# The second norm of a GNN stack: row sums and centred squares in place of the statistics instructions, copies in another order

## What is computed

```python
def _layernorm(x, axis=-1, eps=1e-05):
    m = jnp.mean(x, axis=axis, keepdims=True)
    v = jnp.var(x, axis=axis, keepdims=True)
    return (x - m) / jnp.sqrt(v + eps)
...
    x = _layernorm(x + _L0_gnn_ref(x, adj, ...))     # masked gram matrix, rows scaled to norm 1, times values
    x = _layernorm(x + _L1_gnn_ref(x, adj, ...))     # normalized adjacency times (x @ weight), plus bias
    x = _layernorm(x + _L2_gnn_ref(x, adj, adj, ...))  # three steps of a gated update
    x = _layernorm(x + _L3_gnn_ref(x, adj, ...))     # attention with 8 heads and a mask
```

## Time and profile before

| | us |
|---|---|
| median of 3 runs | 2118.96 |
| lowest and highest | 2114.54 and 2122.32 |
| the profiled execution, its own time | 2114.17 |
| its span, first to last instruction | 2112.4 |

### The profile page before, as it was taken

One profiled execution on the slowest core, in us unless ns is written; L12 is line 12 of the kernel. 1 busy time (PEld: TensorE's weight loads), 2 busy tenths in 40 slices (PEclk: granted clock), 3 DMA queues, 4 the chain that ended last, 5 costly groups with the idle time before them and its releaser, 6 DMA issues.

```text
span 2112.4 us, 34482 instructions
## 1 busy us (share of the span) xinstructions
PE 2027.2 (96%) x12214; PEld 1632.8 (77%) x12214; DVE 1570.5 (74%) x3442; ACT 1253.7 (59%) x2501; POOL 1032.5 (49%) x1153
## 2 busy tenths in 40 slices
PE   6889999999999999999999999999999999999986
PEld 5667787877878787787877878787787877878764
DVE  5567777777777778777777777778777777877756
ACT  3335647566575656646566575656657566565745
POOL 3123645446364554545445463554535555454546
PEclk8999999999999999999999999999999999999999
DMA  4003022120211203112120212213012120302212
GB/s 135 1 20 70 21 51 51 41 71 21 57 35 48 63 22 71 39 41 51 41 71 21 64 27 57 54 31 71 30 41 51 41 71 21 70 21 61 51 47 65
DMA packets 65631, 101.14 MB, mean 48 GB/s; under 512 B 11440, under 2 KB 31152, under 8 KB 65456
## 3 DMA queue, kind: packets, MB, share of 16 engines
q1 hardware_dynamic: 65456, 98.87, 18.4%
HBM read 23.34 MB, written 8.39 MB: 15 GB/s over the span
## 4 chain that ended last, share of the span: by engine, by line
PE 88%; DVE 4%; ACT 3%; POOL 2%; issue 2%; SPq 0%; DMA 0%; POOLq 0%; DVEq 0%; ACTq 0%
PE ps L1026 18%; PE ps L1028 17%; PE ps L1027 17%; PE ps L1048 12%; PE ps L1140 10%; PE ps L1160 6%; PE ps L1124 5%; PE ps L1451 2%; ACT fa L449 1%; POOL fa L334 1%; PE ps L1220 1%; PE ps L1253 1%; POOL rsum L328 1%; DVE ra L943 0%; DVE fa L781 0%
## 5 line engine op out<-in xcount | busy, mean ns | idle before, releaser
L328 POOL TENSOR_TENSOR rsum<-esum,mhalf 128x2 f32<-128x2 f32 x256 | 209.9, 820 | 598.6 <-ACT fa L449 598.5
L334 POOL TENSOR_SCALAR fa<-fa,rsum 128x512 f32<-128x512 f32 x512 | 442.1, 875 | 54.5 <-POOL rsum L328 54.5
L781 DVE CUSTOM_DVE_ANT_0 fa<-ps,mask 128x512 f32<-128x512 f32 x512 | 332.2, 686 | 157.3 <-PE ps L1124 152.0
L449 ACT ACTIVATE fa<-fa,nmax 128x512 f32<-128x512 f32 x512 | 367.0, 725 | 48.2 <-DVE nmax L781 48.2
L444 ACT COPY pT<-ps 128x512 f32<-128x512 f32 x480 | 276.8, 583 | 150.3 <-PE ps L1140 148.5
L1140 PE MATMUL ps<-ident,fa 128*128 128x128 f32 x1920 | 287.2, 275 | 14.6 <-POOL fa L334 10.6
L1140 PEld LDWEIGHTS ps<-ident,fa 128*128 128x128 f32 x1920 | 230.4, 141 | 88.1 <-issue 22.7
L768 DVE TENSOR_TENSOR ra<-ps,ra 128x512 fp32r<-128x512 f32 x224 | 150.9, 686 | 181.8 <-ACT ra L591 94.4
L1048 PE MATMUL ps<-adjT,ra 128*128 128x512 f32 x1024 | 261.2, 405 | 8.0 <-DVE ra L943 5.2
L1048 PEld LDWEIGHTS ps<-adjT,ra 128*128 128x128 f32 x1024 | 192.5, 192 | 63.1 <-ACT pT L444 8.3
L323 POOL TENSOR_TENSOR rstd<-veps,mhalf 128x2 f32<-128x2 f32 x128 | 98.0, 771 | 167.9 <-DVE veps L748 167.9
(11 more groups left out here) (197 smaller groups left out, 4682.8 us busy)
## 6 DMA issues: line engine op xcount, KB each, us to landing
ra<-ra SPq DMA_DIRECT2D x512, 128.0 KB, 2.4
fa<-in_x_T SPq DMA_DIRECT2D x17, 512.0 KB, 4.7
fa<-in_x SPq DMA_DIRECT2D x17, 512.0 KB, 3.9
out<-fa SPq DMA_DIRECT2D x15, 512.0 KB, 3.0
fa<-in_L_gnn_w_w SPq DMA_DIRECT2D x3, 512.0 KB, 10.7
adj_n<-in_adj SPq DMA_DIRECT2D x1, 1024.0 KB, 8.1
fa<-in_L_gnn_u_w SPq DMA_DIRECT2D x2, 256.0 KB, 10.0
out<-xn SPq DMA_DIRECT2D x2, 256.0 KB, 2.1
```

What stands on the lines that cost most here:

```text
L328: nc.gpsimd.tensor_tensor(rsum[:, 2 * k:2 * k + 2], esum[:, 2 * k:2 * k + 2], mhalf[:, 4:6], ALU.pow).then_inc(rs_r, 1)
L334: nc.gpsimd.tensor_scalar(SC[:, g], SC[:, g], rsum[:, 2 * k + u:2 * k + u + 1], 1.0, ALU.mult, ALU.mult).then_inc(nrm, 1)
L449: nc.scalar.activation(SC[:, s % RING], SC[:, s % RING], ACT.Exp, bias=nmax[:, s:s + 1], scale=-1.0, accum_out=esum[:, s:s + 1]).then_inc( ...
L781: nc.vector.tensor_tensor_reduce(out=SC[:, s % RING], in0=ps[:, (4 if i is not None else lone_bank(k)) + u], in1=mask[:, 2 * (k % 8 // 4) ...
```

## The change

The second norm no longer uses the statistics instructions. `sums_and_means` lets the residual sum itself accumulate the row sum (`xsum`), and VectorE makes `nmean` = -sum / (32 D) from it. ScalarE squares x / 32 + `nmean` with an accumulator, four tiles of 128x256 into `XS` (which is free by then), so `vsum` is a quarter of the variance (256 / 1024), and VectorE adds a quarter of eps. VectorE also writes the mean into `mv` for `normalize`. Two semaphores are new: `x2_m` (nmean of a half is there) and `x2_q` (its squares are).

The order around it changes as well:

- TensorE: `qk_of(3)` ahead of `back(t, 0, 0)`; the transposes of x2's first half between `back(t, 0, 0)` and `back(t, 0, 1)`; `back(t, 0, 1)` in bank 6 in place of bank 0, so that it needs the copy of `back(t, 0, 0)`; in this gather, two more node tiles ahead of the wait for bank 1, and no wait for `prob_copy(t, 0, 1)`.
- ScalarE: squares behind `exponentials(t, 0)` and ahead of `qk_hi(2)`; both copies of x2's high words in a row, `qk_hi(3)` behind them, and `prob_copy(t, 0, 1)` behind the copies of `hT` and its high words.
- VectorE: both low-word steps of x2 in a row ahead of `qk_lo(2)`; `qk_lo(3)` behind the low words of hT; the statistics of X4 (batch o) behind the gather's low words of the first step.

```diff
--- before.py
+++ after.py
@@ -65,6 +65,10 @@
         mv = sb("mv", [P, 4, NT, 2])
         veps = sb("veps", [P, 4, NT])
         rstd = sb("rstd", [P, 4, NT])
+
+        xsum = sb("xsum", [P, NT])
+        nmean = sb("nmean", [P, NT])
+        vsum = sb("vsum", [P, NT])
         rsd = sb("rsd", [P, NT])
         ssq = sb("ssq", [P, NT])
         rnorm = sb("rnorm", [P, NT])
@@ -120,7 +124,7 @@
         ps = ctx.enter_context(nc.psum_tensor("ps", [P, 8, N], F32))
         PT_BANK, O_BANK = 6, 7
         QK_BANK = (6, 7, 1, 7)
-        CHAIN_G, CHAIN_T, CHAIN_O = 2 * 6 + 2 + 8 * STEPS, 4, 4
+        CHAIN_G, CHAIN_T, CHAIN_O = 6 + 4 + 2 + 8 * STEPS, 4, 4
 
         def pair(b):
             return ps[:, b:b + 2, :]
@@ -132,10 +136,7 @@
             return slice(2 * c, 2 * c + 2)
 
 
-
         def pt_bank(k, c):
-            if (k, c) == (0, 1):
-                return 0
             return 4 + c if k in (5, 9, 13) else PT_BANK
 
         adj_in = sem("adj_loaded"); w0_in = sem("layer_0_weights_loaded"); w2_in = sem("layer_2_weights_loaded")
@@ -166,6 +167,7 @@
         sq_f = sem("rel_squared"); ssq_ps = sem("ssq_ps"); ssq_c = sem("ssq_copied"); rn_r = sem("rnorm_ready")
         sq_s = sem("squares_summed")
         u_ps = sem("u_ps"); u_h = sem("u_h"); u_l = sem("u_l"); o_ps = sem("o_ps")
+        x2_m = sem("x2_means"); x2_q = sem("x2_squared")
         ln_v = [sem(f"var_of_norm_{k}") for k in range(4)]
         ln_r = [sem(f"rstd_of_norm_{k}") for k in range(4)]
         x1s_f = sem("x1_scaled"); x1s_h = sem("x1s_h"); x1s_l = sem("x1s_l")
@@ -554,15 +556,22 @@
                     tiles_hi(AB0, 0, t_ps, t_h)
                 if t is not None:
                     exponentials(t, 0)
+                if i is not None:
+                    for c in range(2):
+                        act.wait_ge(x2_m, i * 2 + (c + 1))
+                        for s in (2 * c, 2 * c + 1):
+                            ins = nc.scalar.activation(XS[:, s], xg[:, s], ACT.Square, bias=nmean[:, s:s + 1],
+                                                       scale=1.0 / 32, accum_out=vsum[:, s:s + 1])
+                        ins.then_inc(x2_q, 1)
+                if t is not None:
                     qk_hi(2)
                     prob_copy(t, 0, 0)
-                    qk_hi(3)
-                for c in range(2):
-                    if i is not None:
+                if i is not None:
+                    for c in range(2):
                         act.wait_ge(x2_r, i * 2 + (c + 1))
                         copy(XNS[:, H, half(c)], xg[:, half(c)]).then_inc(xn_h, 1)
-                    if t is not None and c == 0:
-                        prob_copy(t, 0, 1)
+                if t is not None:
+                    qk_hi(3)
                 if i is not None:
                     for d in range(DT):
                         act.wait_ge(hT_ps, i * 2 + (d + 1))
@@ -571,6 +580,7 @@
                         act.wait_ge(h_c, i * 2 + (d + 1))
                         copy(HTS[:, H, d], hT[:, d]).then_inc(hT_h, 1)
                 if t is not None:
+                    prob_copy(t, 0, 1)
                     exponentials(t, 1)
 
                 for j in range(STEPS):
@@ -763,6 +773,23 @@
                         after("g", mark("g", ins))
                         variance("g", k, c, aggregate("g", k, c, stats_of("g", xg, k, c)))
 
+
+
+                def sums_and_means():
+                    for c in range(2):
+                        dve.wait_ge(o1_ps, i * 2 + (c + 1))
+                        for s in (2 * c, 2 * c + 1):
+                            ins = STT(xg[:, s], natural(2)[:, s], dinv[:, s:s + 1], xg[:, s], ALU.mult, ALU.add,
+                                      accum_out=xsum[:, s:s + 1])
+                        after("g", mark("g", ins))
+                        TS(nmean[:, half(c)], xsum[:, half(c)], -1.0 / (32 * D), None, ALU.mult).then_inc(x2_m, 1)
+                    for c in range(2):
+                        n = mark("g", TS(mv[:, 1, half(c), 0], xsum[:, half(c)], 1.0 / D, None, ALU.mult))
+                    after("g", n)
+                    for c in range(2):
+                        dve.wait_ge(x2_q, i * 2 + (c + 1))
+                        TS(veps[:, 1, half(c)], vsum[:, half(c)], 0.25 * EPS, None, ALU.add).then_inc(ln_v[1], 1)
+
                 def tile_lo(dst, b, d, ready, value, signal):
                     dve.wait_ge(ready, value)
                     TT(dst[:, L, d], ps[:, b + d], f32(dst[:, H, d]), ALU.subtract).then_inc(signal, 1)
@@ -933,28 +960,24 @@
                     masked(0)
                 if i is not None:
                     dve.wait_ge(xb_r, i + 1)
-                    sums_and_statistics(1, o1_ps, dinv, xg)
+                    sums_and_means()
                 if i is not None:
                     normalize(xg, xg, 1, 0, i, x2_r)
                     normalize(xg, xg, 1, 1, i, x2_r)
-                for c in range(2):
-                    if i is not None:
+                if i is not None:
+                    for c in range(2):
                         dve.wait_ge(xn_h, i * 6 + (c + 1))
                         TT(XNS[:, L, half(c)], xg[:, half(c)], f32(XNS[:, H, half(c)]), ALU.subtract).then_inc(xn_l, 1)
-                    if t is not None and c == 0:
-                        qk_lo(2)
-                if t is not None:
+                if t is not None:
+                    qk_lo(2)
                     masked(1)
-                    qk_lo(3)
                 if i is not None:
                     for d in range(DT):
                         dve.wait_ge(hT_h, i * 6 + (d + 1))
                         TT(HTS[:, L, d], hT[:, d], f32(HTS[:, H, d]), ALU.subtract).then_inc(hT_l, 1)
                 if t is not None:
+                    qk_lo(3)
                     masked(2)
-                if o is not None:
-                    dve.wait_ge(x4a, o + 1)
-                    x4_0, x4_1 = stats_of("o", X4, 3, 0), stats_of("o", X4, 3, 1)
 
                 for j in range(STEPS):
                     A, B_, C, E = [4 * (j + 1) + k for k in range(4)]
@@ -970,6 +993,9 @@
                         m = i * 6 + 2 * j
                         for d in range(DT):
                             tile_lo(AB0, 0, d, a_h, m + (d + 1), a_l)
+                    if o is not None and j == 0:
+                        dve.wait_ge(x4a, o + 1)
+                        x4_0, x4_1 = stats_of("o", X4, 3, 0), stats_of("o", X4, 3, 1)
                     if t is not None:
                         if j == 0:
                             masked(3)
@@ -1054,14 +1080,17 @@
                 node_tile(0, 1)
                 pe.wait_ge(ready, value + 1)
                 if second is not None:
+                    node_tile(0, 2)
+                    node_tile(0, 3, (H,))
                     pe.wait_ge(second, second_value)
                 node_tile(1, 0, (H,))
                 with pe.If(lo_words > 0):
                     for q in range(DT):
                         for s in range(NT):
                             mm(ps[:, q, :], xs[:, H, s, q * P:(q + 1) * P], adjT[:, L, s], start=False, stop=False)
-                node_tile(0, 2)
-                node_tile(0, 3).then_inc(signal, 1)
+                if second is None:
+                    node_tile(0, 2)
+                node_tile(0, 3, (H, L) if second is None else (L,)).then_inc(signal, 1)
                 node_tile(1, 0, (L,))
                 for s in range(1, NT):
                     ins = node_tile(1, s)
@@ -1127,7 +1156,7 @@
                 def back(b, k, c):
                     if c == 0:
                         pe.wait_ge(nrm, b * TILES + (2 * k + 2))
-                    if k == 0:
+                    if k == 0 and c == 0:
                         pe.wait_ge(vv_r, b + 1)
                     elif pt_bank(k, c) == PT_BANK:
                         pe.wait_ge(pt_c, b * TILES + (2 * k + c - (2 if c == 0 and k - 1 in (5, 9, 13) else 0)))
@@ -1345,18 +1374,18 @@
                 if t is not None:
                     score(1)
                     qk_of(2)
-                    back(t, 0, 0)
                     qk_of(3)
-                    back(t, 0, 1)
-                if i is not None:
-                    for s in range(NT):
-                        if s % 2 == 0:
-                            pe.wait_ge(x2_r, i * 2 + (s // 2 + 1))
-                        for d in range(DT):
-                            ins = nc.tensor.transpose(ps[:, 2 + d, s * P:(s + 1) * P], xg[:, s, d * P:(d + 1) * P],
-                                                      ident[:, :])
-                            if s == NT - 1:
-                                ins.then_inc(hT_ps, 1)
+                for c in range(2):
+                    if t is not None:
+                        back(t, 0, c)
+                    if i is not None:
+                        pe.wait_ge(x2_r, i * 2 + (c + 1))
+                        for s in (2 * c, 2 * c + 1):
+                            for d in range(DT):
```

(6 more changed lines are left out.)

## The result

The kernel after takes 2071.06 us (median of 4 runs, 2069.47 to 2072.35), the kernel before 2117.97 (4 runs, 2114.54 to 2122.32): a ratio of 0.978, 95% interval 0.9761 to 0.98. The direction was right, the size wrong by a factor of 2.6.

A forecast was written before the change was run, and what follows sets the result against it. TensorE's queue was taken as the bound, gaining only where it waits around the second norm. 1.05 us a pass x 15 = 15.8, with the first pass together 17, gave 2101 us, range 2088 to 2117.

The forecast's parts named there:

- What bounds: TensorE's queue, busy 96% of the span, is the path; a change gains only where that queue stands still.
- these 2.1 us are all that this place can give: TensorE's waits around the second norm and its gather sum to 2.1 us a pass, 31 us over 15 passes.
- Part 1: TensorE's order: qk_of(3) ahead of back(t,0,0) removes the 0.87 us wait for L334; alone it only moves the wait.
- Part 2: The new norm: squares of 0.50 us each on ScalarE, x2's halves normalized at 1061.65 and 1062.50 us.
- The hold of the means to the end of L334: VectorE's two copies of the mean for half 1 are held until GpSimd's L334 ends at 1059.82 us.
- Part 3: Who follows the norm: gather starts 0.88 us earlier and loses 0.27 us of waiting, so it ends 1.15 us earlier.
- Part 4: Whether the lead is given back: back(t,1,0) costs 0.1 us of it; moving X4's statistics gives 1.3 us of room.
- Sum: 1.05 us x 15 = 15.8, with the first pass together 17 us; 2101 us forecast.
- A: Rival: lead kept whole or better, no holds or squares of 0.4 us; 1.4 to 2.1 us a pass, 2087 to 2098; 15%.
- B: Rival: gain given back at back(t,1,0) through ScalarE's longer queue; 0 to 8 us in all, 2111 to 2119; 17%.
- C: Rival: slower, back(t,0,1) waits for prob_copy(t,0,0) behind the squares; 2128 at 1.1 us a square; 5%.
- D: Rival: the change does not do what it says, the wait is elsewhere, all within noise; 2119; 3%.

The follow-up runs named there:

- e1: The kernel before with one unused tile of 96 bytes a partition ahead of rsd, nothing else: 2098.36 us, ratio 0.9903.
- e3: The kernel after with the statistics instructions put back for the second norm and the squares taken out, new order and placement kept: 2082.71 us, ratio 0.9829.
- g_x4_stats_back: The kernel after with the statistics of X4 back on VectorE ahead of the gather's low words in the first step: 2074.77 us, ratio 0.9793.

## Why the prediction was wrong, step by step

- **What bounds.** Right: TensorE's queue is the path, and the place is the second norm. Wrong: "these 2.1 us are all that this place can give: 31 us over 15 passes". That counted gaps between matmuls and took a matmul's own step (0.235 us) as fixed. 3.8 ns in 330 steps are 1.25 us a pass (e1 alone gained 1.10) and stood in no term, bound or rival: the prediction gave the moved tiles no cost, without a reason. This is the step that failed most: 14 to 21 of the 29 us that were missed.
- **Part 1** held. The wait for L334 is gone in all passes, and alone it mostly moved the wait (e3: 0.83 us a pass gained).
- **Part 2.** Squares 0.50 forecast, 0.51 and 0.49 measured; accumulator reads as priced; `nmean` of half 1 held, 0.56 us measured for 0.40. The hold of the means to the end of L334 was wrong by the rows (0.25 us for two). x2's first half came at 1061.4 on the old scale for 1061.65, so TensorE's wait was 0.70 us for 0.8.
- **Part 3.** The gather's lead at its start was 1.14 us (against e1, of equal placement, by starts in the mean of the steady passes) for 0.88 forecast; its own shortening 0.32 (4.08 to 3.76) for 0.27. Right in kind, a quarter short.
- **Part 4** had the wrong sign. Nothing was given back at `back(t,1,0)`. In its place the statistics of X4, which I had put down as room without a price, were worth 0.29 us a pass by the period (g_x4_stats_back), 0.32 at their place. The rows had said so: 1.40 us on VectorE from 1069.94 on, and the gather's low words behind them are what w4 waits for. In e1 TensorE stands there for 0.32 us.
- **Sum.** 1.05 us a pass for norm and order, measured 1.87 at equal placement (125.10 to 123.23): 27 us for 16 to 17. The 0.82 more are 0.26 + 0.05 in Part 3, 0.1 + 0.32 in Part 4, and 0.09 at the first matmul by `u3` of the second gated step, 54 us behind the gather's start, where the kernels with the new norm lose nothing and e1 and e3 do. In the first pass TensorE's longest wait for x2 went from 4.5 to 3.5 us, where 1.2 were forecast. The median's scale leant on a slip too: one of the three runs of before lay near 2114, not two.
- **The rivals.** A had its size right for norm and order (1.4 to 2.1 us a pass), mostly for another reason: of its conditions only one came true, and that in part, as the means were not held but `nmean` and the variance were, and x2's first half came 0.2 us before its forecast. B and C did not occur. D (no effect) did not. What did was on no list.
- The two parts of the change need each other. On equal placement the norm alone is worth 1.6 us, the order alone 15.7, both 27.3. For the norm, one instruction's place on ScalarE (`qk_hi(3)`) is worth 13.4.

## What to carry to other kernels

When a change adds or resizes a tile, look up what moved behind it, and time the old kernel with an unused tile of that size before anything is put down to the change; 96 idle bytes were worth a third to a half of this one. On a path that one engine bounds, multiply its commonest instruction by the smallest change of step that you can imagine: 330 a pass times 4 ns outweighed every wait in the list. And follow a result that comes earlier through each queue it must pass: it was held up by an instruction in front of it that waited for another engine.

## What was not expected of the hardware

The rate of float32r matmuls depends on where the stationary and the moving operand lie in SBUF, and for the weights' 128x512 matmuls on their distance: 230 ns with `ra` and the weights both shifted by 128 bytes (h_adjT_at_64), 232.4 with `ra` alone shifted (h_movers_at_64). The gather's 128x512 matmuls took 227.4 ns at a distance of a multiple of 1024 bytes and 233 at 32, 64, 128, 928 and 992 beyond one; 128x256 matmuls took 113.7 to 119.9 ns over the same layouts, with no rule found. The granted clock was 1.00 (the 2.4 GHz level) in all these stretches. Small VectorE steps on 128x2, 0.17 us when alone, behaved differently beside two GpSimd instructions in a row of 0.69 us each: one took 0.56 us and ended with the first of them, the next two took 0.25 together, and one took 0.48 and ended with the second.
